# The sum of base and nbeta goes from VectorE in the message pass to GpSimd in the last node pass

## The reference, cut to what matters

```python
x = x + _L0_gnn_ref(...)                   # x2 = x + relu(second relational level)
h = jnp.maximum(_layernorm(x), 0.0)
# _L1_gnn_ref(h, ...):
msg = layer_norm(relu(relu(edge_input @ eW1 + eb1) @ eW2 + eb2), eg, ebeta)
node_agg = segment_sum(msg, receivers)
upd = relu(concat([h, node_agg]) @ nW1 + nb1) @ nW2 + nb2
x = x2 + layer_norm(h + upd, ng, nbeta)    # (h + upd - mean) * rstd * ng + nbeta
```

## Time and profile before

| | |
|---|---|
| median of 3 runs | 2752.02 us (2725.98 to 2770.67) |
| profiled execution, its own time | 2723.2 us |
| its span | 2721.5 us |
| DVE busy | 2027.0 us (74%), 6853 instructions |
| POOL busy | 1789.8 us (66%), 1381 instructions |
| E3, POOL's first gather to its last scatter | about 1769 to 2442 us |
| N3, SP's first load to the end | about 2448 to 2721 us |

### The profile page before, as it was taken

How to read it: one execution, slowest core, us unless ns; L and a number is a source line. 1 busy time by engine, 2 the same in 40 slices (tenths; PEclk the granted TensorE clock), 3 DMA queues, 4 the chain that set the end, 5 groups by cost and what they waited for, 6 DMA issues and landing times. The chain is left out here.

```text
span 2721.5 us, 54736 instructions
## 1 busy us (share of the span) xinstructions
PE 2137.1 (79%) x16219; PEld 1872.3 (69%) x16219; DVE 2027.0 (74%) x6853; ACT 1542.8 (57%) x3284; POOL 1789.8 (66%) x1381
## 2 busy tenths in 40 slices
PE   5778999999588899888881666477777776749997
PEld 5678999999588798888881555445544444426675
DVE  7888888888233677676654888688778787737999
ACT  7996666666233444444443787544444444427887
POOL 7773777776676288888866777568888888860000
PEclk9998999999799999999996888889888898879999
DMA  8994555555399444454536999867777777749998
GB/s 282 321 311 127 96 103 106 108 107 103 79 353 366 150 74 74 79 82 79 84 46 185 415 417 412 327 217 208 196 203 195 204 191 206 187 77 359 407 408 340
DMA packets 296008, 563.74 MB, mean 207 GB/s; under 512 B 88627, under 2 KB 145376, under 8 KB 295904
## 3 DMA queue, kind: packets, MB, share of 16 engines
q1 hardware_dynamic: 186144, 484.03, 51.4%
q0 software_dynamic: 109760, 78.51, 18.2%
HBM read 368.35 MB, written 205.52 MB: 211 GB/s over the span
## 5 line engine op out<-in xcount | busy, mean ns | idle before, releaser
L1078 POOL DMA_INDIRECT s<-E_summed,c_scat x392 | 637.8, 1627 | 250.9 <-issue 101.7
L1307 PE MATMUL ps<-c_w,E_masked 128*128 128x128 f32 x6272 | 720.3, 276 | 3.9 <-DVE E_masked L1110 3.8
L1307 PEld LDWEIGHTS ps<-c_w,E_masked 128*128 128x128 f32 x6272 | 711.7, 193 | 4.7 <-DVE E_masked L1110 4.7
L1110 DVE SCALAR_TENSOR_TENSOR E_masked<-E_type_row,E_hT 128x512 f32<-128x512 int32 x784 | 484.0, 688 | 79.0 <-ACT E_hT L1227 65.5
L368 POOL DMA_INDIRECT gathered<-s,c_src x392 | 419.0, 1069 | 167.3 <-issue 115.8
L1439 POOL DMA_INDIRECT s<-E_summed,c_scat x196 | 339.9, 1734 | 83.3 <-issue 58.2
L1429 POOL DMA_INDIRECT E_ends<-h,c_near x196 | 201.7, 1029 | 79.7 <-issue 56.4
L368 POOL DMA_INDIRECT gathered<-in_x,c_src x196 | 189.2, 965 | 70.3 <-issue 59.1
L587 PE MATMUL ps<-c_sl,N_hT 128*128 128x128 f32 x1568 | 196.7, 279 | 19.4 <-DVE N_out L409 17.4
L1322 PE MATMUL ps<-E_msg,E_same 128*128 128x128 bf16 (+1 forms) x2450 | 207.3, 241 | 1.2 <-DVE E_msg L1160 1.2
L587 PEld LDWEIGHTS ps<-c_sl,N_hT 128*128 128x128 f32 x1568 | 184.9, 194 | 28.1 <-ACT N_hT L534 20.2
(11 more groups left out here) (133 smaller groups left out, 4387.4 us busy)
## 6 DMA issues: line engine op xcount, KB each, us to landing
s<-N_out SPq DMA_DIRECT2D x147, 512.0 KB, 5.0
N_xin<-in_x SPq DMA_DIRECT2D x98, 512.0 KB, 10.2
N_sin<-s SPq DMA_DIRECT2D x98, 512.0 KB, 6.8
E_dst_row<-in_dst_line SPq DMA_DIRECT2D x147, 256.0 KB, 4.8
E_type_row<-in_type SPq DMA_DIRECT2D x98, 256.0 KB, 4.1
N_xin<-s SPq DMA_DIRECT2D x49, 512.0 KB, 6.2
h<-N_h SPq DMA_DIRECT2D x49, 512.0 KB, 7.8
E_base<-s SPq DMA_DIRECT2D x49, 512.0 KB
```

Source lines behind the costliest of these rows:

```text
L1078: pool.indirect_dma_start(s, bass.IndirectOffsetOnAxis(ap=c["scat"][:, k:k + 1], axis=0), summed[:, g % 2, t * D:(t + 1) * D], None, bound ...
L1110: nc.vector.scalar_tensor_tensor(out=masked[:, u % 2, r, :], in0=type_row[:, u, :], scalar=float(r), in1=hT[:, u % 2, :], op0=ALU.is_equal ...
L1307: ins = nc.tensor.matmul(ps[:, 2 + u % 2, t * D:(t + 1) * D], masked[:, u % 2, r, t * P:(t + 1) * P], w[:, r, :], start=(r == 0 and t == 0 ...
```

## The change

The add of `nbeta` leaves DVE's step in E3. The base that E3 stores is then x2 alone; the store waits for one step (`g + 1`) rather than two. In N3 POOL gets a program of its own: for each of the 49 groups it waits until the base has landed, adds `nbeta` in place (one instruction of 128x1024 floats, both inputs in SBUF), and raises the same semaphore by one, so that DVE's `finish` waits for 17 per use of a buffer, 16 by the transfer and 1 by POOL. `B_RING` is 2, so the base still has two buffers, as before; the condition under which SP loads a base is as it was.

```diff
@@ node_pass_3
+    B_RING = 2
-    base = sb("N3_base", [P, 2, NT * D])
+    base = sb("N3_base", [P, B_RING, NT * D])
...
+        @block.gpsimd
+        def _(pool):
+            for g in range(GROUPS_N):
+                u = g % B_RING
+
+                pool.wait_ge(based[u], 17 * (g // B_RING) + 16)
+                nc.gpsimd.tensor_tensor(tiles_of(base[:, u, :]), tiles_of(base[:, u, :]), each_tile(c["nbeta"], NT),
+                                        ALU.add).then_inc(based[u], 1)
+
...
-                    dve.wait_ge(based[u], 16 * (g // 2 + 1))
+                    dve.wait_ge(based[g % B_RING], 17 * (g // B_RING + 1))
...
-                nc.vector.tensor_tensor(res[:, u, cols], scaled[:, cols], base[:, u, cols],
+                nc.vector.tensor_tensor(res[:, u, cols], scaled[:, cols], base[:, g % B_RING, cols],
@@ edge_pass_messages
-                sp.wait_ge(base_step, 2 * g + 2)
+                sp.wait_ge(base_step, g + 1)
...
-            def add_nbeta(i, u):
-
-                dve.wait_ge(base_step, 2 * (UNROLL * i + u) + 1)
-                nc.vector.tensor_tensor(tiles_of(base[:, u % 2, :]), tiles_of(base[:, u % 2, :]),
-                                        each_tile(c["nbeta"], NT), ALU.add).then_inc(base_step, 1)
...
                 update(i, u)
-                add_nbeta(i, u)
                 message_variances(i, u)
```

More of the change, by code:

```diff
@@ L818, in node_pass_3 @@
     loaded = [S(f"loaded{k}") for k in range(UNROLL)]
-    based = [S(f"based{k}") for k in range(2)]
+    based = [S(f"based{k}") for k in range(B_RING)]
     stored = [S(f"stored{k}") for k in range(2)]
@@ L843, in load_base @@
             def load_base(g):
-                u = g % 2
+                u = g % B_RING
                 wait(sp, out_ready, 2 * (g - 1))
@@ L857, in _ @@
                 load(g)
-            for g in range(2):
+            for g in range(B_RING):
                 load_base(g)
```

## The result

The changed kernel takes 2771.41 us in the median of 20 runs, the kernel before 2724.97 in the median of its 20 (the three shown ahead of the prediction lie high among them). The ratio is 1.0171, with a 95% interval of 1.0142 to 1.02: slower, but by less than 2%. The profiled execution has a span of 2760.4 us, 38.9 more than before. It splits by DVE's first `finish` in N3, at 2471.5 us before and 2464.1 after: 7.4 us are gained ahead of it, and from there to the end it takes 296.3 us rather than 250.0, 46.3 more. (This execution took 2762.2 us, 9 us under the median of its kernel, and the one before only 2 us under.

A forecast was written before the change was run, and what follows sets the result against it. POOL's queue was taken to bound E3 and DVE to bound N3. E3's -12 us and the collision's +30 us made +18 us on the median of 2752.0, so 2770 us, with a range of 2725 to 2840 for 8 in 10.

The forecast's parts named there:

- E3, -12 us: In E3, POOL's scatters and gathers no longer lose time to DVE's `add_nbeta`: -12 us, ends 0 and -55.
- The 15 and the 10 us: Two estimates of E3's gain: 15 us by `add_nbeta`'s share of long two-input instructions, 10 us by counting scatters under it.
- The add, 1.9 us: In N3, POOL's add of 128x1024 was taken as 1.9 us, between 1.03 and 4.5 us.
- The estimate of 2.25 us: POOL's add in N3, as half the page's 4497 ns for 2048 columns; would make the collision cost 38 us.
- The wait, 0 to 0.1 us: In N3, DVE's wait for the base with POOL's add in the chain: nothing or 0.1 us a group.
- the 2.0 us of cover: In N3, time left for POOL's add between the base's landing and the `finish` that needs it.
- The collision, +30 us: In N3, POOL's add keeps DVE's next two-input instruction from starting: period 5.8 against 5.16 us, +30 us over 48 groups.
- the formula: N3's group period as (3.97 + landing time + add time) / 2, predicted 5.8 us.
- rival 2: In N3, DVE loses the whole add in every group: +79 us in all, 2831 us; chance 0.25.
- The sum: Whole kernel: -12 in E3 and +30 in N3 make +18 us, put on the median of 2752.0.
- Rival 1: In N3, no collision, POOL and DVE run side by side: -12 us, 2740 us; chance 0.20.
- Rival 3: E3 gives more, POOL's rhythm meeting almost no DVE block: up to -55 us with N3 free, 2697; chance 0.07.

The follow-up runs named there:

- e1: Changed kernel with POOL's add of nbeta in N3 left out altogether; ratio 0.9955 against the kernel before.
- e8: Kernel before, with `add_nbeta` in E3 replaced by two 512-column copies from PSUM to a spare tile (nbeta left out); ratio 0.9996.
- e10: Kernel before, all work kept, `update` and `add_nbeta` in E3 each split into four instructions of 256 columns; ratio 0.9947.
- e4: Changed kernel with three buffers for the base in N3 and its load one group earlier; ratio 1.0191 against the kernel before.
- e9: Changed kernel, POOL filling a spare tile instead of adding nbeta, and N3's L158 multiplying by an SBUF tile of halves; ratio 1.001 against before.
- e6: Changed kernel with three base buffers, POOL's add waiting until the statistics of its group are through; ratio 1.0421 against the kernel before.
- e11: e7 with `update` in four parts and the steps with `eg` and `ebeta` in two; 2700.0 us against 2720.8 before, ratio 0.9916.
- e7: Changed kernel, three base buffers, DVE's four half-tile instructions given one SBUF input each through PSUM, add placed after DVE's shifts; ratio 0.9992 against before.

## Why the prediction was right

2770 us were predicted, 2771.41 measured, and the case that came is the forecast's. That the two numbers lie so close is luck, though; the mechanism is not. By the steps:

- *E3, -12 us.* 9 us in the mean of the profiles, 12 by e1. That POOL bounds E3 and DVE's 60 us are worth nothing showed in the wait for `E_msg` and in e1; that POOL lost its time to the block, in e8's and e10's scatters. The 15 and the 10 us that I had weighed enclose it.
- *The add, 1.9 us.* Mis-sized: it takes 2.36 us alone (2.43 in the mean with what it waits for DVE). Two passes at the pace of the earlier trace rows are too little for it. The estimate of 2.25 us by the page GPSIMD Engine Reference of the Trainium skill was nearer.
- *The wait, 0 to 0.1 us.* Right: DVE never waits for the base in N3, and a third buffer is no use (e4). But with an add of 2.36 us the 2.0 us of cover would not have been enough had DVE been on time: e9 shows 7.7 us of waiting and a period of 5.38.
- *The collision, +30 us.* The mechanism, its victim (the first two-input instructions behind the statistics) and the landing (5.7 against 5.8 us) were right. The size was 46: with the measured 2.43 and 5.8 the formula gives (3.97 + 5.8 + 2.43) / 2 = 6.10 us, and 6.1 was measured. The step behind the formula, that DVE loses what lies behind 2.9 us, would give the add's start plus 4.62 us; the rounds show the start plus 4.46, as L150 ends with the add (2533.87 against 2533.84) instead of beginning its own 0.17 us behind it. What the formula left out is that landings vary (4.0 to 10.2 us): no steady place is reached, three adds catch a `finish` for nearly their whole length, which was rival 2 group by group, and twelve are held by DVE.
- *The sum.* +18 predicted, +39 in the profile and +46 between medians. The size of the change was taken at less than half. The absolute time came out by luck, since the three runs shown ahead lay 27 us above the median of 20 and the two misses cancelled.
- *Rival 1* fell with L150's 969 ns. *Rival 2* is real where the place makes it so (e6, 1.0421). *Rival 3*, E3 losing far more of its block, did not come by the change; but part of that time can be had, as e10 and e11 gain 14 and 25 us of E3 by shorter DVE instructions (e11 also without `add_nbeta`).

## What to carry to other kernels

Before work goes to an idle GpSimd, list the VectorE instructions it will lie beside. Here those with two SBUF inputs stood until GpSimd's add ended, and a VectorE without slack lost 0.96 us per 2.4 us add. Put under work that reads PSUM, by a wait at the right place, the same add cost N3 nothing (e7). Where GpSimd's queue is the bound, as in E3, cutting long two-input VectorE instructions in pieces shortened the stage (e10).

## What the runs showed of the hardware

- The exclusion is by instruction and works both ways: DVE's L152 (8 columns) stood 2.33 us under POOL's add of 2.36; 13 scatters that started 0.1 to 0.4 us into DVE's 1.22 us instruction took 2.24 to 2.54 us instead of 1.54. The page SBUF — State Buffer of the Trainium skill (Who interferes with whom) states the first half, for a GpSimd instruction that reads SBUF, and the trace agrees. For indirect transfers it differs: the section infers that `tensor_tensor` does not hold up the making of their descriptors, while here the scatter is held by one (2.24 us against 1.55), and the measurement decides.
- A POOL memset blocks a DVE `tensor_scalar` from SBUF to SBUF (877 against 171 ns in the mean) and no `tensor_tensor` (L150 at 173 ns). This agrees with the same section of the Trainium skill, SBUF — State Buffer (Who interferes with whom).
- DVE's record of a blocked instruction shows the block as its own length (L150 at 969 ns), not as idle time: DVE's busy share, 284.68 of 292 us, did not tell that anything was wrong.
- An add of 128x1024 float32 on POOL takes 2.36 us, on DVE 1.22.
